# A graph layer on one core: the edge stage's second layers feature-major, the product turned back, the scatter in two matmuls

## The reference

```python
gates = ssp(edge_state @ We1 + be1) @ We2 + be2
soft_cutoff = 1.0 - jax.nn.sigmoid(5.0 * (edges_distance - (CUTOFF - 1.5)))
gates = gates * soft_cutoff
h = ssp(nodes @ Wn1 + bn1) @ Wn2 + bn2
messages = h * gates
message_sum = jnp.zeros_like(node_state).at[edges[:, 1]].add(messages)
new_state = node_state + (ssp(message_sum @ Ws1 + bs1) @ Ws2 + bs2)
```

## Time and profile before

| what | value |
|---|---|
| device time, median of 3 runs | 1993.46 us (1991.19 to 1993.70) |
| profiled execution, its span | 1988.8 us |
| what lies around the span, by the median | 4.7 us |
| PE, ACT, DVE, POOL busy | 87%, 77%, 65%, 75% of the span |
| mean granted TensorE clock | 0.949 |
| DMA | 157.78 MB, mean 79 GB/s |

### The profile page before, as it was taken

The page is one execution under the profiler, slowest core; times in us unless marked ns, Lnnn a source line. Parts: engine busy times, 40 slices in busy tenths (PEclk is TensorE's granted clock), DMA queues, the critical chain, the costliest instruction groups (busy, mean ns, idle before and its releaser), DMA issues.

```text
span 1988.8 us, 53540 instructions
## 1 busy us (share of the span) xinstructions
PE 1737.7 (87%) x16249; PEld 1328.7 (67%) x16249; DVE 1285.6 (65%) x3512; ACT 1532.1 (77%) x3368; POOL 1484.7 (75%) x1572
## 2 busy tenths in 40 slices
PE   4699999898888988878889988998988898988987
PEld 3577777676666666666666766766666676766666
DVE  4578888666665655555656666666666666666666
ACT  3589999777777777777777788788777787787877
POOL 7777777777777777777777777777777777777773
PEclk7799999999999899999989999899999899999999
DMA  5433333333333333333333333333333233333331
GB/s 122 122 85 98 97 97 97 85 85 76 91 74 73 71 73 70 75 68 71 74 71 74 74 80 74 74 75 78 74 75 75 69 84 75 75 78 75 75 76 38
DMA packets 256432, 157.78 MB, mean 79 GB/s; under 512 B 45401, under 2 KB 227046, under 8 KB 256366
## 3 DMA queue, kind: packets, MB, share of 16 engines
q1 hardware_dynamic: 202652, 104.94, 18.2%
q0 software_dynamic: 50048, 51.35, 15.5%
q10 hardware_dynamic: 3666, 0.68, 0.2%
HBM read 146.94 MB, written 9.87 MB: 79 GB/s over the span
## 4 chain that ended last, share of the span: by engine, by line
POOL 57%; issue 22%; PE 11%; DVE 3%; ACT 2%; SPq 2%; DMA 2%; DVEq 1%; ACTq 1%; POOLq 0%
POOL ga L459 57%; PE ps L623 3%; PE ps L636 3%; PE ps L640 1%; DVE hid L1113 1%; SPq L340 1%; PE ps L585 1%; DMA ga<-in_x_dram,srcT 1%; PE ps L575 1%; DVE hid L1117 1%; PE ps L653 1%; PE ps L662 1%; PE ps L577 0%; DVEq L1139 0%; ACT lg L861 0%
## 5 line engine op out<-in xcount | busy, mean ns | idle before, releaser
L459 POOL DMA_INDIRECT ga<-in_x_dram,srcT x1564 | 1483.7, 949 | 477.6 <-issue 472.4
L852 ACT ACTIVATE lg<-ps,bn1c 128x512 f32<-128x512 f32 x391 | 268.4, 687 | 306.6 <-PE ps L585 267.6
L636 PE MATMUL ps<-wn,hid 128*128 128x64 f32 x3128 | 447.9, 288 | 18.9 <-DVE hid L1117 17.1
L1113 DVE SCALAR_TENSOR_TENSOR hid<-ps,neg_b,lg 128x512 f32<-128x512 f32 x391 | 292.8, 749 | 221.9 <-ACT lg L867 205.2
L636 PEld LDWEIGHTS ps<-wn,hid 128*128 128x128 f32 x3128 | 393.1, 197 | 51.5 <-DVE hid L1117 26.6
L575 PE MATMUL ps<-ident,ea 128*128 128x128 f32 x782 | 173.8, 305 | 198.2 <-DMA ga<-in_x_dram,srcT 135.2
L844 ACT COPY xe<-ps 128x512 f32<-128x512 f32 x391 | 229.9, 588 | 113.3 <-PE ps L577 99.8
L623 PE MATMUL ps<-xe,wn 64*128 64x256 f32 x1564 | 289.8, 449 | 0.0
L1151 DVE TENSOR_TENSOR acc<-acc,ps 64x64 f32 x782 | 168.4, 215 | 163.7 <-issue 157.9
L640 PE MATMUL ps<-we,hid 128*128 128x128 f32 x1564 | 273.1, 299 | 0.0
L575 PEld LDWEIGHTS ps<-ident,ea 128*128 128x128 f32 x782 | 80.0, 143 | 282.1 <-issue 268.8
(11 more groups left out here) (124 smaller groups left out, 1847.9 us busy)
## 6 DMA issues: line engine op xcount, KB each, us to landing
ea<-in_edge_attr_dram SPq DMA_DIRECT2D x195, 256.0 KB
ga<-in_x_dram,srcT POOLq DMA_INDIRECT x1564
bw<-b_tab SPq DMA_DIRECT2D x782, 32.0 KB
relb<-rel_tab SPq DMA_DIRECT2D x196, 64.0 KB
b_tab<-share SPq DMA_DIRECT2D x25, 250.0 KB
out_dram<-xs SPq DMA_DIRECT2D x25, 125.0 KB
xs<-in_x_dram SPq DMA_DIRECT2D x3, 750.0 KB
rows_i<-in_dst_dram SPq DMA_DIRECT2D x1, 768.0 KB
```

The costliest lines, as they stand in the source:

```text
L459: pool.indirect_dma_start(to[:, t % 2, t // 2, :], None, x, bass.IndirectOffsetOnAxis(ap=idx[:, t:t + 1], axis=0)).then_inc(done, 16)
L636: pe.matmul(hg[:, t * D:(t + 1) * D], hid[:, u % 2, t * P:(t + 1) * P], wn2[:, :], start=False, stop=False, skip_group_check=True)
L852: act.activation(lg[:, u % 2, 0:QUAD].rearrange("p (k e) -> p k e", k=2), z[:, :, 0:PAIR], ACT.Abs, bias=bn1c[:, 0:1]).then_inc(n_abs, 1)
L1113: dve.scalar_tensor_tensor(out=hid[:, u % 2, 0:QUAD].rearrange("p (k e) -> p k e", k=2), in0=ps[:, 2 * (u % 2):2 * (u % 2) + 2, 0:PAIR], s ...
```

## The change

The second layers are turned round: `mid` now holds the weights stationary (`wn2`, and `we2` as a block-diagonal 128x128) and moves the edges, 256 columns at a time, two matmuls of 64 output rows for the hidden part and one of 128 for the gates. The result is feature-major in PSUM (`ps_hid`, `ps_gate`). ACT no longer fills a bank with biases; `gates_out` copies the gates to SBUF with their bias. DVE's `product` adds the hidden part's bias and multiplies by the gates. PE turns the product back to edge-major (`turn_back`, two transposes), and DVE's `message` reads that, multiplies by the cutoff and writes `msg`, so that both halves k lie side by side. The scatter `back` is now two matmuls of 128 output rows and 128 columns, of which the diagonal blocks are used. `gates_in` is two matmuls with a block-diagonal 128x128 `we1`. PE's order in a step is `front(s)`, `transposes(s+2)`, `mid(s-1)`, `turn_back(s-2)`, `back(s-3)`; DVE's is `hidden(s-1)`, `message(s-3)`, `one_hot(s-1)`, `flush(s-4)`, `product(s-2)`, `pick(s+2)`; ACT's ends with `gates_out(s-1)`. TensorE records go from 40 to 28 a quad.

```diff
-        gcut = sb("gcut", [P, 2, PAIR])
-        msg = sb("msg", [P, 2, 4, D])
+        gate = sb("gate", [P, PAIR])
+        prod = sb("prod", [P, PAIR])
+        msg = sb("msg", [P, 2, 2, 2, D])
...
-        ps_hg = [ps[:, 6, :], ps[:, 5, :]]
+        ps_hid = [ps[:, 5 + n, PAIR:2 * PAIR] for n in range(2)]
+        ps_gate = [ps[:, 5 + n, 0:PAIR] for n in range(2)]
+        ps_m = ps[:, 7, P:P + PAIR]
...
             def gates_in(u, slot):
-                for j in range(2):
-                    half = slice(j * D, (j + 1) * D)
-                    for k in range(2):
-                        mm = pe.matmul(ps[k * D:(k + 1) * D, 2 * (u % 2) + j, PAIR:PAIR + P], we1[half, :],
-                                       xe[half, slot, 0, k * P:(k + 1) * P], start=True, stop=True)
+                for k in range(2):
+                    mm = pe.matmul(ps[:, 2 * (u % 2) + k, PAIR:PAIR + P], we1[:, :], xe[:, slot, 0, k * P:(k + 1) * P],
+                                   start=True, stop=True)
                 return mm
...
-            def mid(q, u, hg):
+            def mid(q, u, n):
 
                 pe.wait_ge(hid_b, q + 1)
-                pe.wait_ge(filled, q + 1)
-                for t in range(4):
-                    pe.matmul(hg[:, t * D:(t + 1) * D], hid[:, u % 2, t * P:(t + 1) * P], wn2[:, :],
-                              start=False, stop=False, skip_group_check=True)
-                gates = hg[:, PAIR:2 * PAIR].rearrange("p (k j d) -> p k j d", k=2, j=2)
+                if reached(q, 2):
+                    pe.wait_ge(prod_b, q - 1)
+                units = hid[:, u % 2, 0:QUAD].rearrange("p (k j e) -> p j k e", k=2, j=2)
                 for j in range(2):
-                    mm = pe.matmul(gates[:, :, j, :], hid[:, u % 2, QUAD + j * P:QUAD + (j + 1) * P],
-                                   we2[:, :].rearrange("p (k d) -> p k d", k=2),
-                                   start=False, stop=(j == 1), skip_group_check=True)
+                    pe.matmul(ps_hid[n][j * D:(j + 1) * D, :].rearrange("d (k e) -> d k e", k=2), wn2[:, :], units[:, j],
+                              start=True, stop=True)
+                mm = pe.matmul(ps_gate[n], we2[:, :], hid[:, u % 2, QUAD:QUAD + PAIR], start=True, stop=True)
                 mm.then_inc(hg_mm, 1)
 
+            def turn_back(q):
+
+                pe.wait_ge(prod_b, q + 1)
+                for k in range(2):
+                    mm = pe.transpose(ps_m[:, k * P:(k + 1) * P], prod[:, k * P:(k + 1) * P], ident[:, :])
+                mm.then_inc(prod_t, 1)
+
             def back(q, u, sums=ps_s):
 
-                pe.wait_ge(oh_b, q + 1 if isinstance(q, int) and q == NQ - 1 else q + 2)
+                pe.wait_ge(oh_b, q + 1)
                 pe.wait_ge(msg_b, q + 1)
                 if reached(q, 1) and sums is ps_s:
                     pe.wait_ge(flushed, q)
                 for j in range(2):
-                    for k in range(2):
-                        mm = pe.matmul(sums[k * D:(k + 1) * D, 0:W], msg[:, u % 2, 2 * k + j, :],
-                                       oh[:, u, 2 * k + j, :], start=(j == 0), stop=(j == 1))
+                    mm = pe.matmul(sums[:, 0:2 * W].rearrange("f (k w) -> f k w", k=2),
+                                   msg[:, u % 2, j, :, :].rearrange("e k d -> e (k d)"), oh[:, u, j:4:2, :],
+                                   start=(j == 0), stop=(j == 1))
                 mm.then_inc(sc_mm, 1)
...
                 if not known or s + 2 < NQ:
                     transposes(s + 2, (v + 2) % ARING)
+                if not known or 1 <= s <= NQ:
+                    mid(s - 1, (u - 1) % RING, (u - 1) % 2)
+                if not known or s >= 2:
+                    turn_back(s - 2)
                 if not known or s >= 3:
                     back(s - 3, (u - 3) % RING)
-                if not known or 1 <= s <= NQ:
-                    mid(s - 1, (u - 1) % RING, ps_hg[(u - 1) % 2])
...
+                front(NQ - 1, (NQ - 1) % ARING)
+                mid(NQ - 2, (NQ - 2) % RING, (NQ - 2) % 2)
+                turn_back(NQ - 3)
+                back(NQ - 4, (NQ - 4) % RING)
                 pe.wait_ge(flushed, NQ - 1 - BACK)
                 node_hidden(NG - 2, ps_h_end)
-                mid(NQ - 1, (NQ - 1) % RING, ps_hg[(NQ - 1) % 2])
+                mid(NQ - 1, (NQ - 1) % RING, (NQ - 1) % 2)
+                turn_back(NQ - 2)
+                back(NQ - 3, (NQ - 3) % RING)
+                node_out(NG - 2, ps_y_end)
+                turn_back(NQ - 1)
                 back(NQ - 2, (NQ - 2) % RING)
-                node_out(NG - 2, ps_y_end)
                 back(NQ - 1, (NQ - 1) % RING, ps_s_end)
...
-            def fill(q, hg, ring):
-
-                if reached(q, ring):
-                    act.wait_ge(msg_b, q - (ring - 1))
-                act.copy(hg, bsum[:, :, :, :].rearrange("p h k d -> p (h k d)")).then_inc(filled, 1)
+            def gates_out(q, n):
+
+                act.wait_ge(hg_mm, q + 1)
+                if reached(q, 1):
+                    act.wait_ge(prod_b, q)
+                act.activation(gate[:, :], ps_gate[n], ACT.Identity,
+                               bias=bias2[:, 1:2]).then_inc(gate_e, 1)
...
                 logs(q, u)
-                fill(q, ps_hg[u % 2], 2)
+                if not isinstance(q, int) or q >= 1:
+                    gates_out(q - 1, (u - 1) % 2)
...
-                    fill(q, ps_hg[q % 2], 2)
+                    gates_out(q - 1, (q - 1) % 2)
                     if node is not None:
                         node_step(*node)
+                gates_out(NQ - 1, (NQ - 1) % 2)
                 node_sizes(NG - 2, ps_h_end)
...
-                if reached(q, 2):
-                    dve.wait_ge(sc_mm, q - 1)
+                if reached(q, RING):
+                    dve.wait_ge(sc_mm, q - (RING - 1))
...
-            def message(q, u, hg, scattered=sc_mm):
-                dve.wait_ge(hg_mm, q + 1)
-                dve.tensor_tensor(gcut[:, u % 2, :].rearrange("p (t d) -> p t d", d=D),
-                                  hg[:, PAIR:2 * PAIR].rearrange("p (t d) -> p t d", d=D),
-                                  cutT[:, quad_cols(q)].unsqueeze(2).broadcast_to([P, 4, D]),
-                                  ALU.mult).then_inc(gc_b, 1)
-                dve.wait_ge(gc_b, q + 1)
-                if scattered is not None:
-                    if reached(q, 2):
-                        dve.wait_ge(scattered, q - 1)
-                dve.tensor_tensor(msg[:, u % 2, :, :].rearrange("p t d -> p (t d)"), hg[:, 0:PAIR],
-                                  gcut[:, u % 2, :], ALU.mult).then_inc(msg_b, 1)
+                    in1=lg[:, u % 2, QUAD:QUAD + PAIR].rearrange("p (k e) -> p k e", k=2), op0=ALU.max, op1=ALU.add).then_inc(hid_b, 1)
+
+            def product(q, n):
+
+                dve.wait_ge(gate_e, q + 1)
+                dve.scalar_tensor_tensor(out=prod[:, :], in0=ps_hid[n], scalar=bias2[:, 0:1], in1=gate[:, :],
+                                         op0=ALU.add, op1=ALU.mult).then_inc(prod_b, 1)
+
+            def message(q, u, scattered=sc_mm):
+
+                dve.wait_ge(prod_t, q + 1)
+                if scattered is not None and reached(q, 1):
+                    dve.wait_ge(scattered, q)
+                dve.tensor_tensor(msg[:, u % 2, :, :, :].rearrange("p j k d -> p k j d"),
+                                  ps_m.rearrange("p (k j d) -> p k j d", k=2, j=2),
+                                  cutT[:, quad_cols(q)].rearrange("p (k j) -> p k j", k=2).unsqueeze(3).broadcast_to(
+                                      [P, 2, 2, D]), ALU.mult).then_inc(msg_b, 1)
...
+                if not known or s >= 3:
+                    message(s - 3, (u - 3) % RING)
+                if not known or 1 <= s <= NQ:
+                    one_hot(s - 1, (u - 1) % RING)
+                if not known or s >= 4:
+                    if at is None or at == 0:
+                        load_places(s - 4, 1 if at is None else RING)
+                    flush(s - 4, at or 0)
                 if not known or 2 <= s <= NQ + 1:
-                    message(s - 2, (u - 2) % RING, ps_hg[(u - 2) % 2])
+                    product(s - 2, (u - 2) % 2)
                 if node is not None:
                     node_step(*node)
                 if not known or s + 2 < NQ:
                     pick(s + 2, (u + 2) % RING)
-                if not known or 1 <= s <= NQ:
-                    one_hot(s - 1, (u - 1) % RING)
-                if not known or s >= 3:
-                    if at is None or at == 0:
-                        load_places(s - 3, 1 if at is None else RING)
-                    flush(s - 3, at or 0)
...
-                load_places(NQ - 3, 3)
-                message(NQ - 2, (NQ - 2) % RING, ps_hg[(NQ - 2) % 2])
+                message(NQ - 3, (NQ - 3) % RING)
+                one_hot(NQ - 1, (NQ - 1) % RING)
+                load_places(NQ - 4, 4)
+                flush(NQ - 4, 0)
```

(23 more changed lines are left out.)

52 lines of the change are left out of this document (25 added, 27 removed).

## The result

The changed kernel takes 2000.6 us (median of 4 runs, 2000.02 to 2000.92) against 1992.33 us for the kernel before (median of 4 runs, 1990.35 to 1993.70). The ratio is 1.0039, 95% interval 1.0027 to 1.0052: 8.3 us slower. The profiled execution took 2000.92 us, 2.0 us around its span.

A forecast was written before the change was run, and what follows sets the result against it. POOL's gathers were taken to bound the kernel, so only the tail counted: span 1988.8 + 3.6 order + 1.4 clock = 1993.8, + 4.7 around the span = 1998.5 us, 0.25% slower; range 1993 to 2018.

The forecast's parts named there:

- The bound: POOL's queue of gathers, never free, sets the pace at 4.99 us a quad; the change does not touch it.
- Rival 1: PE side becomes the bound, its loop with half clock over 4.895 us a quad: 2028 us at 4.97; chance 0.25.
- Rival 2: Tail costs only 2.5 us, hidden(390) starting before 8.2 and the clock full: 1996 us, no change; chance 0.30 with a paced run.
- T: Start of the last transposes, after the last gather: 1964.64 us before, forecast to stay within 1 us.
- Rival 3: Gathers themselves get cheaper as other engines touch memory less; 6 ns each needed to end at 1989; chance 0.06.
- TensorE's own work: PE's records in a quad: 2.29 us removed, about 2.3 added, so a step stays at 3.9 to 4.4 us.
- The tail: Work behind the last gather: node_hidden(24) 3.6 us later through the order of work, plus 1.4 us for the clock.
- k: Start of node_hidden(24) behind the last transposes, in the tail: 12.7 us before, forecast 16.3.
- Clock: PE's clock drop in the tail: may come ahead of node_hidden(24), costing another 2.0 us if so; taken as 1.4.
- The places: DVE's reading of places every fourth step, now ahead of the product on the loop: 1.55 us per four quads.
- The clock in the loop: PE now waits in every quad, so more half clock was expected: mean clock under 0.949, hidden beside the gathers.
- Around the span: Time outside the profiled span, up to the median 1993.46: 4.7 us, added to the forecast span.

The follow-up runs named there:

- the filler: Changed kernel with 13 extra identity matmuls, results unread, in PE's two longest gaps of the tail: 6.6 us above its kernel before.
- e1: Changed kernel with DVE's last hidden layer ahead of one-hot, places and flush in the tail: ratio 1.0034 on a slow chip; repeated elsewhere, 5.6 us above its kernel before.

## Why the prediction was right, and where its sizes were off

**The bound** was read rightly. The pitch is that of before, the last gather starts at 1961.89, and neither 12 records fewer nor a slower PE side moves the end. Rival 1 (PE side the bound) did not come, and with half the gathers one sees by how much: in the steps that count longest the PE side has 0.3 us of room a quad. It caught up with the gathers at quad 115 instead of 66, and what it was late until then was free. Rival 2 (cheaper tail, 1996) did not come either: hidden(390) started 9.75 us behind T, not before 8.2. Rival 3 did not: the mean of a gather is 948 ns (949 before).

**TensorE's own work.** The prediction left a quad at 3.9 to 4.4 us for fewer records; from one quad's transposes to the next at full speed it is 1961.81 - 1957.79 = 4.02 us (3.94 before).

**The tail** is the term that was mis-sized: 3.6 us of order and 1.4 of clock were predicted. With the clock held by the filler k is 18.18, so order is 18.18 - 12.68 = 5.5 us, and the clock is the other 2.7; 8.2 in all.
- Order, as predicted and as measured in the changed kernel, us behind T: `node_hidden(23)` 6.4 and 6.87; hidden(390) 8.6 and 9.75; `mid(390)` 9.75 and 10.94. The steps come in the order that was written down. Up to here it is 1.2 us: `message(388)` came at 7.14 instead of 6.45, since the count let scatter 387 end where it in fact starts, and reading the places cost 1.36 us of standing where 1.0 was taken. Behind it, with the clock held: the node's sum 14.3 where 12.8 was counted, `node_hidden(24)` 18.2 where it was 16.3; some 0.7 us more in all, spread over the links.
- Clock: the prediction priced a drop at `node_hidden(24)`, +2.0 us. That record group hardly feels it: 2.13 us at half (1987.28), and 1.94 (1973.25) or, in the kernel before, 2.05 at full. The drop came 10 us sooner, ahead of `mid(390)`, whose 1.05 us from the count became 2.07 up to the next group, and every short group behind it (scatter 1.19 instead of 0.68) was on the path. The filler shows 2.7 us for it.

Cut another way, the 8.2 us are 2.7 of clock, 1.8 that DVE's order in the tail gave back (e1), and 3.7 that no experiment took out. What stands there in the order of work is the gates copied to SBUF, the product, the product turned back, and the message, one after another, where there was one gate and one message before; that these links are the 3.7 us is argued from the order, not shown. The prediction's 3.6 us is near this 3.7 by chance: it held DVE's late hidden layer too.

**T** was to stay within 1 us. It moved 1.74 us, because PE stood 1.99 us behind the last gather instead of 0.04 ahead of it. The last node group holds PE up just ahead of the end (4.9 us behind at quad 385), and with the slower step it then recovers 0.6 us a quad, where the kernel before recovered 0.8. In the changed kernel and the four that differ from it in the tail alone T lies between 1965.9 and 1968.0, always above 1964.6, and PE is 1.9 to 2.0 us behind the last gather in each. This is the one place in which the loop's pace reached the end.

**The places** on the loop were priced at 0.4 us a quad; they cost next to nothing there (plain steps 4.315 us against a count of 4.2 without them and 4.6 with them; the share and node steps came to 4.65 and 4.68 where 4.8 and 4.7 were counted). The prediction took an idle engine in the old order as the cost of the instruction in any order.

**The clock in the loop** was to be below 0.949, since PE would wait in every quad. It does, and the clock was full from 110 us to 1973 us (1.00), while it had been 0.96 in the mean from 110 to 1950 before. The step that failed is "now PE waits in every quad, so I expect more of it". PE is idle for about as long as before (188 of 1840 us, 198 before), but in other pieces: 36.0 us in 64 waits for the hidden layer, 21.9 in 89 for the product and 103.8 in 124 for gathers, where it was 17.1 in 49 for the hidden layer and 135.2 in 142 for gathers. Counted in the traces between 110 and 1950 us, 32 gaps of PE were 1.5 us or longer before, 11 of them 1.8 or longer; now they are 9 and 1. That the shorter gaps are why the clock holds fits the tail, where a gap of 2.13 us lost it, but is only argued; no run varied it in the loop.

**Around the span** 4.7 us were carried over, the difference of one profiled execution to a median of others. In the four executions of the changed kernel the time is 2.0 to 2.3 us more than the span. By that the profiled execution of before took some 1991 us (an estimate), 2.4 below its median, which is also why the spans differ by 10.1 us and the medians by 8.3. The median of 2000.6 is 1.7 us above the profiled span, so this term took 3.0 us back from the miss of 5.1 in the span (1998.9 against 1993.8) and left 2.1 in the time. The bound was read rightly; that the number came so near its forecast is partly luck, two errors against each other.

What stays open: why some chips take 27% longer, and whether four tiles side by side were what `gates_in` lost.

## What to carry to other kernels

Find the queue that is never free and ask of each edit whether it touches that queue; here three tenths fewer TensorE records, and a PE side that is 6% slower by itself, change nothing up to the last transfer, and there 2 us. Then follow the new dependencies once through the tail, behind the last transfer, where nothing hides the depth of the pipeline: a new link is no longer covered, and neither is the clock that falls in the gaps between links: 8.2 us here. A cost seen as idle time belongs to its place in the queue, so price a moved instruction by what the queue can overlap at the new place.

## What the runs showed of the hardware

- From 110 to 1950 us a granted clock of 1.00 with PE 90% busy, and 0.96 in the kernel before with PE 89% busy; the busy share alone did not tell the one from the other.
- A record group whose duration hardly depends on the clock (`node_hidden`, 1.94 to 2.05 us at full and 2.13 at half) beside groups that nearly double (0.65 and 1.12; 0.68 and 1.19).
- The full clock lost within one idle time of PE of 2.13 us (1.00 up to 1976.4, 0.63 from there to 1977.0, 0.50 from 1977.3), and kept where filler matmuls or another order made that gap short.
- The kernel before at 1992, 2510 and 2537 us on different chips. On the slowest, engines stood still together for 2 to 5 us at a time: around 1200.8 us of e1 DVE had waited 4.21, ACT 5.20 and POOL 2.42 us, all released by "remote". With half of the gathers a kernel ran at its usual pace on the chip on which the full one took 2510 us.
- Reading eight values into a queue's registers takes 0.60 us in the median of the changed kernel and 1.84 in that of before, where the reading stands at another place of DVE's queue.
